# Signalling a tile's products by a drain of TensorE instead of by its last matmul, in the second pass of a sparse graph layer

## The reference

```python
h = jnp.maximum(_layernorm(x), 0.0)
e = leaky_relu(h @ a[:F] + (h @ a[F:]).T, 0.2)
U = softmax(where(adj > 0, e, -9e15), axis=1)
prop_u = U @ h
rowsum = sum(U * 0.5 * U, axis=1)
xi = h * rowsum[:, None]
feat = coe[2] * (prop_u - xi) + (1 - coe[2]) * (h + prop_u - xi)   # then a soft threshold
pu = U @ feat
# out = x + a mix, by gates, of feat, pu, rowsum and h0
```

## Time and profile before

| What | Value |
|---|---|
| median of three runs | 1512.9 us |
| lowest, highest | 1499.7, 1515.14 us |
| the profiled execution, its own time | 1488.81 us |
| its span, first to last instruction | 1487.2 us |
| mean granted TensorE clock | 0.808 |
| PE, DVE, ACT, POOL busy | 953.7, 932.0, 863.0, 602.7 us |

### The profile page before, as it was taken

How to read it: one execution, slowest core, us unless ns; L and a number is a source line. 1 busy time by engine, 2 the same in 40 slices (tenths; PEclk the granted TensorE clock), 3 DMA queues, 4 the chain that set the end, 5 groups by cost and what they waited for, 6 DMA issues and landing times.

```text
span 1487.2 us, 27559 instructions
## 1 busy us (share of the span) xinstructions
PE 953.7 (64%) x3629; PEld 576.7 (39%) x3630; DVE 932.0 (63%) x5233; ACT 863.0 (58%) x1840; POOL 602.7 (41%) x649
## 2 busy tenths in 40 slices
PE   3545776776676767667777777764266456565665
PEld 2521254443443433333334433332145344343433
DVE  7756556776778878888888888877511222323433
ACT  4673677877788888888888888881222121111111
POOL 1004354443333323322222222215566676666664
PEclk9975689889889888997887787876568777877778
DMA  6989887999999999999999999952344454555665
GB/s 182 358 288 370 335 319 276 336 339 349 353 347 353 378 368 372 371 379 387 374 384 376 366 380 378 371 208 69 87 123 127 120 164 138 162 172 179 191 193 160
DMA packets 146214, 415.70 MB, mean 280 GB/s; under 512 B 29166, under 2 KB 109054, under 8 KB 129782
## 3 DMA queue, kind: packets, MB, share of 16 engines
q1 hardware_dynamic: 115868, 345.65, 62.8%
q0 software_dynamic: 30304, 69.62, 15.0%
HBM read 398.37 MB, written 33.90 MB: 291 GB/s over the span
## 4 chain that ended last, share of the span: by engine, by line
DVE 31%; issue 25%; PE 15%; DMA 6%; another core or an unknown queue 5%; POOL 5%; ACT 4%; POOLq 4%; DVEq 3%; ACTq 1%; SPq 0%
PE TP L321 4%; PE ACC L689 3%; POOL W L634 3%; DVE XHO L1068 2%; PE ACC L693 2%; DMA W<-feat_d,IDT 2%; PE MISC L989 2%; POOLq L623 2%; DMA R<-in_x_dram 1%; ACT SG L309 1%; DMA R<-sc_d 1%; POOL R L634 1%; DVEq L257 1%; DVE JK L1135 1%
## 5 line engine op out<-in xcount | busy, mean ns | idle before, releaser
L309 ACT ACTIVATE SG<-W,ABOVE 128x4096 bf16<-128x4096 f32 x126 | 467.0, 3706 | 77.4 <-DVE cnt L1051 46.9
L634 POOL DMA_INDIRECT R<-haug_d,IDS x230 | 229.8, 999 | 598.2 <-issue 583.0
L321 PE MATMUL TP<-SG,FOLD 128*128 128x512 bf16 x1008 | 304.3, 444 | 0.0
L680 ACT ACTIVATE DG<-ident,WSR 128x128 f32<-128x128 f32 x230 | 76.1, 391 | 338.2 <-remote 181.4
L1777 DVE SCALAR_TENSOR_TENSOR R<-ACC,SELF,R 128x256 f32<-128x256 f32 x63 | 30.5, 484 | 279.3 <-remote 184.1
L688 PE MATMUL ACC<-XHO,ZB 128*128 128x256 bf16 x126 | 40.5, 321 | 217.1 <-ACTq L682 78.5
L634 POOL DMA_INDIRECT W<-feat_d,IDR x140 | 141.4, 1010 | 73.3 <-issue 73.3
L689 PE MATMUL ACC<-R,DG 128*128 128x256 f32 x446 | 162.3, 515 | 1.5 <-issue 1.5
L321 PEld LDWEIGHTS TP<-SG,FOLD 128*128 128x128 bf16 x1008 | 114.6, 122 | 114.4 <-issue 54.5
L689 PEld LDWEIGHTS ACC<-R,DG 128*128 128x128 f32 x446 | 105.0, 252 | 21.6 <-issue 3.0
L688 PEld LDWEIGHTS ACC<-XHO,ZB 128*128 128x128 bf16 x126 | 12.7, 101 | 249.7 <-issue 124.1
(11 more groups left out here) (295 smaller groups left out, 2286.4 us busy)
## 6 DMA issues: line engine op xcount, KB each, us to landing
W<-in_adj_dram SPq DMA_DIRECT2D x128, 2048.0 KB, 13.3
haug_d<-R POOLq DMA_DIRECT2D x8, 1056.0 KB, 9.7
HTS<-haug_d SPq DMA_DIRECT2D x64, 132.0 KB
R<-in_x_dram SPq DMA_DIRECT2D x8, 1024.0 KB, 6.5
R<-feat_d SPq DMA_DIRECT2D x32, 256.0 KB
R<-in_x_dram SPq DMA_DIRECT2D x32, 256.0 KB
R<-in_L_gnn_h_dram SPq DMA_DIRECT2D x32, 256.0 KB
feat_d<-FTS SPq DMA_DIRECT2D x63, 128.0 KB
```

Of the source, the lines that this page charges most:

```text
L309: nc.scalar.activation(SG[:, u, half(h)], W2[:, u, half(h)], ACT.Sign, scale=2.0 ** 100, bias=ABOVE[:], accum_out=DEG[:, u, h:h + 1]).then ...
L321: nc.tensor.matmul(KP[u], FOLD[:, b], SG[:, u, b * FW:(b + 1) * FW], start=False, stop=False)
L634: pool.indirect_dma_start(out=g[:, k, 0:w], out_offset=None, in_=table, in_offset=bass.IndirectOffsetOnAxis(ap=ids[:, k:k + 1], axis=0), * ...
L680: nc.scalar.mul(DG[:, u, k], ident[:], weights[:, k:k + 1])
```

## The change

In `other_products`, where `between` is given (the second pass alone), the tail matmul no longer increments `prod2_ready` (`done`). A drain of TensorE is put behind it, and the drain increments the semaphore. The first pass is as before. Tile 0's own first signal (`own().then_inc(prod2_ready, 1)`) is as before too. No other instruction moves.

```diff
             if between:
                 between()
-            nc.tensor.matmul(ACCS[u], rw, g[:, KR, 0:F], start=False, stop=True).then_inc(done, 1)
+                nc.tensor.matmul(ACCS[u], rw, g[:, KR, 0:F], start=False, stop=True)
+                pe.drain().then_inc(done, 1)
+            else:
+                nc.tensor.matmul(ACCS[u], rw, g[:, KR, 0:F], start=False, stop=True).then_inc(done, 1)
```

## The result

The changed kernel takes 1544.6 us (median of 4 runs, 1541.5 to 1548.3), the kernel before 1506.3 us in the same series (4 runs, 1497.0 to 1515.1). The ratio is 1.0275, with a 95% interval of 1.0233 to 1.0317: slower by 2.3 to 3.2%, or about 41 us. The profiled execution of the changed kernel took 1547.4 us with a span of 1545.8 us. In the changed file the drain is L697, and the lines behind it stand 3 further on: the finishing addition is L1780 (it was L1777), the wait on the gather count L1723 (it was L1720).

The account below looks back on a forecast made before the run. The tail's late signal, opening gaps between POOL's gathers, was taken to bound the second pass. Gains of 18 us in its first half and 2 in its second gave 1512.9 - 20 = 1493 us, range 1456 to 1560.

Parts of the forecast that it names:

- "Covered" in the first half: Second pass, first half: POOL needs 7.1 us a tile, PE with preparation 6.3, so POOL's gathers cover the preparation.
- hidden in 36 of 62 places: Between tail and next L688: preparation of 1.6 us exposed only in the 26 places following at once, 42 us of PE time.
- The drain itself ... 3 us at most.: PE's drain behind each tail: 0.05 us over the work before it, for 63 tiles 3 us at most.
- Prompt signals close half of the gaps.: First half of the second pass: prompt signals close half of POOL's 35.7 us of gaps between gathers, gaining 18 us.
- A drain's signal is prompt where a matmul's is late.: Slow stretches, second pass: a drain's signal needed at most 4.6 us where a matmul's needed 10.2.
- The weak joint: The drain's promptness in slow stretches was inferred from ScalarE's drain L682 for tile 13, not from a drain of PE.
- The second half: Second pass from 1343 us: PE with preparation bounds at 4.5 us a tile, 135 us against 140; 2 us gain taken.
- The second rival: Between tail and L688: PE's preparation becomes the bound if over 37 of 63 tiles find gathers landed; +42 us, 1555; chance 0.16.
- The third rival: At the tail's drain: held by late matmul completion, PE loses the next tile's products in 22 waits; +84 us, 1597; chance 0.12.

Follow-up runs that it names:

- silent drain: Kernel before, with the tail matmul still signalling and a drain that signals nothing put behind it in the second pass; 1543.9 us against 1499.2, ratio 1.0266.
- stop without a drain: Kernel before, no drain; behind each tail product, which signals as before, PE's sequencer waits for that same signal; 1528.5 us against 1491.9, ratio 1.0256.
- experiment 4: The change, with the signalling drain moved behind PE's two readings (slots, gather count) for the next tile; 1528.7 us, ratio 1.0160 to the kernel before.
- experiment 3: Slot count read three times instead of once per second-pass tile: without drain 1519.8 us against 1489.5, ratio 1.0176; with the change's drain 1614.2 against 1499.2, ratio 1.0750.

## Why the prediction was wrong

The forecast was a gain of 20 us; it was a loss of 41 us. The sign failed in two steps, the cost of the stop and the gain from prompt signals.

- **"Covered" in the first half, hidden in 36 of 62 places.** This is the main step that failed. The size of the preparation was somewhat low: 1.6 us a tile was forecast, and from the end of the drain to the next L688 there are 1.90 us. The exposure was wrong. It was read from the kernel before: 26 of 62 places follow at once, the others wait for gathers, diagonals or L1777, "and the preparation hides in that". Those waits were not a fixed cover. When PE came later to each tile, its gathers had landed (waits for them 102 us before, 6.3 us after), the cover was gone, and all 62 places paid. The comparison of 7.1 us for POOL with 6.3 us for PE in the first half treated POOL's time a tile as given by its gathers alone; yet POOL too waits for PE through the tiles' additions and stage(t+4). With drains in tiles 1 to 31 alone the kernel lost 16 us where a gain was forecast.
- **"The drain itself ... 3 us at most."** This term was read from one quiet drain. Where the release is prompt it is right (0.02 us a tile), but PE was held for 70.9 us over the 62 gaps, 67.0 of them in tiles 1 to 31. So on PE's side the stop made 117.5 us of preparation and 70.9 us of holding, 188.4 us, where the kernel before had gaps of 137.8 us for all reasons. In tiles 1 to 31 either part alone (58.0 or 67.0 us) is less than the 85.4 us of gaps that stood there before; the runs don't say how much of the loss there is due to each.
- **Prompt signals close half of the gaps.** The lags fell as hoped, 243 to 84 us. POOL's gaps rose from 54.3 to 97.6 us. The forecast took a lag to be lost time, but the kernel before does the next tile's products in it. A lag costs only what it delays beyond the next tile.
- **"A drain's signal is prompt where a matmul's is late."** The weak joint, ScalarE's drain at 1202.20, did not bear. The silent drain and the stop without a drain gave the same short lags with the matmul's increment. Where a release was late, the drain was late with it, by 17.2 us in tile 1. What shortens the lags is a stop of PE's sequencer right at the tail. Why it does is not shown: a stop that comes two readings later (experiment 4) leaves 197.5 us of lags, and two more readings without any stop (experiment 3) bring them from 243.3 to 182.0 us, so it may be that PE runs ahead less or only that it comes later to each tile.
- **The second half.** Forecast 4.5 us a tile, 135 us for 30 tiles. From the L688 of tile 32 (1367.78) to that of tile 63 (1537.75) the changed kernel takes 170.0 us for 31 tiles, 5.5 us each; the kernel before 149.5 us, 4.8 each. The forecast was 2.9 us of PE's work and 1.6 us of preparation; measured are 3.45 us from L688 to the tail (3.14 before, at the higher clock) and gaps of 2.05 us.
- **The second rival** was right in place, price and condition: +42 us forecast, +41 measured, all 62 gaps at 1.5 us or more, gathers landed in at least 61 of 63 tiles when PE was ready. The arithmetic behind it, 101 us less 59 of closed gaps, was lucky: POOL's gaps did not close but grew, and PE's gaps grew by 50.6 us because 117.5 us of preparation and 70.9 us of holding took the place of 137.8 us that had been there already. The holding was the third rival's and no part of this one.
- **The third rival** is part of the truth. PE sits through 67.0 of the 125.0 us of gaps in tiles 1 to 31, and through 3.9 of 63.4 us in tiles 32 to 62. Its price of 84 us was too high, since only 12 tiles are held and not 22 or more.

The rule weighed in the prediction ("PSUM — Partial Sum Buffer" of the Trainium skill, section "Engine vs sequencer instructions": the increment belongs on the matmul, a drain waits until the engine is idle) gave the right advice: only the cost was left. Its second part fits the trace where the drain ends 0.02 us behind the tail product. Of its first part, that the increment comes at completion, the trace can't tell: the matmul was heard over 1 us behind its modelled end in 36 of 63 tiles. "Perfetto Trace Analysis" of the Trainium skill, section "Tensor Engine Instruction (MATMUL, LD_WEIGHTS)", says that a matmul's end in the profile is an estimate and that the signal follows the acknowledged writes. The held drains would fit a completion that comes late, but equally a signal that is delivered late; nothing here separates the two.

**Open**: why releases come late. Shown is that it is neither the instruction that signals, nor SyncE's loads or the gathers' volume alone, and that it fades when PE's sequencer stops right at each tile's last products. The traces hold one more regularity, which no run tests. In 10 of the changed kernel's 12 late tiles the addition starts 1.6 to 2.7 us behind the end of a run of POOL's gathers (each within 1 us of the one before); in tile 1 the run's last gather ends at 1115.20 and the held drain at 1117.1. That suggests that releases wait for POOL to pause, and does not show it, since POOL's next gathers themselves wait for the release. A smaller number of gathers was not tried, as each tile's slots need theirs. No version was faster than the kernel before.

## What to carry to other kernels

A drain, or any wait of an engine for its own last instruction, costs the preparation that its sequencer used to do ahead, and, as here, the wait for every release that comes late; price it in every iteration, not only where the engine now follows at once, because idle time in which it would hide is often made by the engine's own early arrival and goes when it arrives later. A long wait by an engine with little to do is no evidence of lost time: ask what the producer does meanwhile, and watch the gap between the producer's iterations. Where a change both moves a signal and stops a sequencer, measure the stop alone: it may account for all that is seen.

## What the runs showed of the hardware

- A drain of PE behind a finished array can be held: 17.2 us past the end of the tail product as modelled in tile 1, 6.0 to 8.1 us in five other tiles; the matmul's increment in the kernel with the silent drain was over 1 us late in as many tiles (12).
- Behind a prompt stop, the addition on VectorE starts 0.24 us after the tail product with a signalling drain, 0.22 us with the matmul's increment and a wait.
- Two more readings of a slot count into PE's sequencer behind a drain put L688 back by 1.25 us a tile and cost 1.13 us a tile of the time. One such reading in the chain above (from 1482.17 to 1482.88) takes 0.71 us.
- Taking the readings out of the stop (experiment 4) raised the time for which the drain was held by over 1 us from 69.0 to 177.5 us.
- Sequencer steps of 0.70 us in the whole program fell from 436 to 153 with the stops, with no change to the other engines' programs.
